# Second attention: the place of the weighted-values matmuls within a step of four scores

## What is computed

```
q, k = rope(h @ Wq), rope(h @ Wk);  v = h @ Wv
scores = q k^T / 4, masked so that row i sees columns <= i
ctx    = softmax(scores) @ v        # softmax subtracts the row maximum
```

## Time and profile before

| | |
|---|---|
| median of 3 runs | 4165.04 us (4164.26 to 4166.23) |
| profiled execution | 4157.04 us, of it the span 4155.2 us |
| PE busy | 3078.5 us, 74% |
| DVE busy | 2298.0 us, 55% |
| ACT busy | 1675.9 us, 40% |
| exponentials of the second attention (L660) | 1536, busy 693.8 us |
| reductions of the maxima (L925) | 1024, busy 733.9 us |
| weighted values (L1254) | 3072 matmuls, busy 327.3 us |

### The profile page before, as it was taken

The page is one execution under the profiler, slowest core; times in us unless marked ns, Lnnn a source line. Parts: engine busy times, 40 slices in busy tenths (PEclk is TensorE's granted clock), DMA queues, the critical chain, the costliest instruction groups (busy, mean ns, idle before and its releaser), DMA issues. The chain is left out here.

```text
span 4155.2 us, 54042 instructions
## 1 busy us (share of the span) xinstructions
PE 3078.5 (74%) x17636; PEld 1799.8 (43%) x17637; DVE 2298.0 (55%) x4488; ACT 1675.9 (40%) x3702; POOL 1106.6 (27%) x972
## 2 busy tenths in 40 slices
PE   5588558765965696579657955885587599999991
PEld 3444434343434443443444343444343366666660
DVE  4775567466837672866386557755675122222225
ACT  2456254525542554256335624562455122222223
POOL 6310630072016202420332053106200222222222
PEclk9789789887988898889788988997789799999995
DMA  1000000000000000000000000000000533333335
GB/s 55 11 11 12 22 21 2 13 20 21 2 30 3 21 2 32 0 21 2 32 1 21 2 32 11 12 12 22 11 2 11 185 55 55 55 61 56 55 53 167
DMA packets 85960, 125.57 MB, mean 30 GB/s; under 512 B 11600, under 2 KB 70864, under 8 KB 83664
## 3 DMA queue, kind: packets, MB, share of 16 engines
q1 hardware_dynamic: 59216, 85.40, 6.5%
q0 software_dynamic: 26496, 37.01, 5.0%
HBM read 58.23 MB, written 63.36 MB: 29 GB/s over the span
## 5 line engine op out<-in xcount | busy, mean ns | idle before, releaser
L660 ACT ACTIVATE PR<-SP_ 128x512 f32<-128x512 f32 (+3 forms) x1536 | 693.8, 489 | 457.8 <-PE SP_ L1241 310.9
L925 DVE TENSOR_REDUCE NM<-MX 128x1 f32<-128x128 f32 (+7 forms) x1024 | 733.9, 752 | 231.2 <-PE MX L1210 221.0
L421 POOL DMA_INDIRECT scratch_xs<-FX,SLOT x128 | 123.7, 967 | 1467.1 <-issue 1465.5
L439 POOL TENSOR_TENSOR work<-QK,VS 128x2048 f32<-128x2048 f32 x128 | 466.6, 3670 | 136.4 <-DVE QK L774 136.2
L1238 PE MATMUL SP_<-work,KST 99*128 99x512 bf16 (+3 forms) x1536 | 469.0, 333 | 44.1 <-ACT PR L660 32.2
L1208 PE MATMUL MX<-KST,work 96*128 96x512 bf16 (+3 forms) x1536 | 442.8, 353 | 70.0 <-DVE NM L925 58.5
L1503 POOL DMA_INDIRECT scratch_h<-Y,XG x136 | 210.6, 1548 | 617.1 <-DVE Y L1566 522.9
L1544 DVE TENSOR_TENSOR AG<-UB,SL 128x512 f32<-128x512 f32 x136 | 94.0, 691 | 476.3 <-PE UB L1583 476.3
L1254 PE MATMUL OA<-PR,V 128*32 128x512 f32 (+3 forms) x3072 | 327.3, 498 | 3.3 <-ACT PR L660 3.3
L1521 ACT ACTIVATE SL<-GB 128x512 f32<-128x512 f32 x136 | 81.2, 597 | 602.3 <-PE GB L1583 602.3
L818 DVE TENSOR_REDUCE AT<-work 128x256 f32<-128x4096 f32 x64 | 282.9, 4420 | 2.2
(11 more groups left out here) (253 smaller groups left out, 5092.7 us busy)
## 6 DMA issues: line engine op xcount, KB each, us to landing
XG<-scratch_xs SPq DMA_DIRECT2D x136, 130.0 KB, 2.1
X<-in_L_attn_x SPq DMA_DIRECT2D x8, 1024.0 KB, 5.6
scratch_x<-X SPq DMA_DIRECT2D x8, 1024.0 KB, 3.9
scratch_h<-A SPq DMA_DIRECT2D x8, 1024.0 KB, 3.9
X<-scratch_x SPq DMA_DIRECT2D x16, 512.0 KB, 4.0
HH<-scratch_h SPq DMA_DIRECT2D x16, 512.0 KB, 4.5
out<-X SPq DMA_DIRECT2D x16, 512.0 KB, 3.1
wg<-in_L_ffn_Wg SPq DMA_DIRECT2D x1, 4096.0 KB, 16.7
```

Source lines behind the costliest of these rows:

```text
L439: sg["prod1"].by(pool.tensor_tensor(P1[t % 2][:, i * hh * D:(i + 1) * hh * D].rearrange("p (h e d) -> p h e d", h=hh, e=HD), QK[:, t % 3, ...
L660: sg["exp"].by(act.activation(PR[:, n % 8, q0:512], SP_[:, n % 2, q0:512], ACT.Exp))
L925: sg["mx"].by(dve.tensor_reduce(NM[:, qt, h:h + 1], src, AX.X, ALU.max, negate=True))
```

## The change

The call of `weighted_values` in PE's list moves from behind the step's second score, ahead of the quarter M1, to behind its fourth score, ahead of M3. Before, the order in a step is: score, M0, score, weighted values, M1, score, M2, score, M3. After it, it is: score, M0, score, M1, score, M2, score, weighted values, M3. No other list changes and nothing is added or removed; the lists of DVE, ACT and SP are as they were.

```diff
                     for h in range(G):
                         scores(u, kt, h)
-                        if h == 1 and k >= 1:
+                        if h == 3 and k >= 1:
                             weighted_values(k - 1, *order[k - 1])
                         maxima(actions[n * h // G:n * (h + 1) // G])
```

## The result

The changed kernel takes 4326.75 us (median of 4 runs, 4325.24 to 4328.85) against 4164.94 us before, a ratio of 1.0387 with a 95% interval of 1.0375 to 1.0399. The direction was as predicted, the size was not: +162 us where +52 was forecast, and far above the range.

What follows compares the result with a forecast made beforehand. Bound by the PE-ACT-PE round with two score banks, and PE-DVE-PE where crowded. Terms (a) to (e) sum to +6.5 us per batch, x 8 = +52, giving 4209 profiled and 4217 us median; range 4172 to 4248.

Steps and rivals of the forecast that it cites:

- What bounds the kernel, and a step's length: Second attention: bound by the PE-ACT-PE round with two score banks, plus PE-DVE-PE where crowded; 2.88 us per step without maxima.
- The closed form: Step after: 1.89 + 1.00 + M3 + turn-over + M0 and M1's excess above 0.66 us; equal to before without maxima.
- (c): Units' first steps: DVE's copy of the sum, and reductions queued behind it, come later and PE waits; +6.8 us per batch.
- (e): Last step: its weighted values leave the gap where ACT idles and lie beside the last exponentials; -0.5 us per batch.
- (b): Units' second steps: the turn-over's four transposes now share the weighted values' gap and cost their full length; +1.9 us per batch.
- The clock: PE through the phase: keeps the full 2.4 GHz although waits grow to at most 1.4 us; nothing added.
- Rival D: The clock falls for some 8 steps a batch at some 1.2 us each: 77 us more, 4294 us; chance 0.05.
- (d): Steps where DVE idled for pieces: M1 and M2 no longer stand behind the weighted values; -3.45 us per batch.
- (a): Steps with a large piece, mostly in M3: it now shares the weighted values' gap; +1.75 us per batch.
- The prediction's own sign of being wrong: Phase not 4 to 10 us longer: the copy's delay is taken up, or (d) is far greater than in step 6.

Runs made afterwards that it cites:

- e1: Changed kernel with six extra matmuls on PE behind the weighted values of steps 4, 16 and 28; 4275.51 us, ratio 1.0298.
- e9: Changed kernel with six extra matmuls in steps 4, 16 and 28, and six ahead of M1 in steps 13 and 25; 4271.23 us, ratio 1.0260.
- e3: Kernel before, weighted values moved behind the fourth score only in the first step of each unit but the first; 4247.41 us, ratio 1.0221.
- e4: Kernel before, weighted values moved behind the fourth score in all steps but the first of each unit; 4219.04 us, ratio 1.0157.
- e5: e4 with the turn-over moved from the end of a unit's second step to behind M1 of that step; 4195.60 us, ratio 1.0069.
- e2: Kernel before with six extra matmuls behind the weighted values of steps 4, 16 and 28; 4185.19 us, ratio 1.0072.
- e7: Changed kernel with the weighted values behind the third score in every step, half the move; 4278.28 us, ratio 1.0273.
- e6: e4 with M3 ahead of the weighted values instead of behind them; 4194.82 us, ratio 1.0066.
- e10: Kernel before with the first action of each two-action step moved from M1 to M2; 4146.16 us, ratio 0.9950.

## Why the prediction was wrong, point by point

*What bounds the kernel, and a step's length*: right. The round without maxima is 2.88 us, step 41 of the first batch 3.38 where 3.32 was predicted; steps 17 and 29 at full clock are 3.76 (e1, e9) where the closed form gives 1.89 + 1.00 + 0.44 + 0.44 = 3.77. The closed form is for steps whose queues hold no other wait, and most of what follows is about those.

*(c), DVE's copy and what is queued behind it, +6.8*: right in place, too small in one part. (c) counted for steps 13 and 25 also M3 and the turn-over behind the weighted values, so e9 is its measure, with the whole move and the clock up: +7.9 us, of it 1.25 in step 4, 2.41 in steps 12 and 13 (for 1.7), 1.34 in step 16, 1.53 in 24 and 25, 1.34 in 28. e3 has 6.6 without that stacking; e4 has 1.0 for steps 13 and 25 alone, of which e5 takes back 0.6 with the turn-over.

*(e), the last step, -0.5*: right, -0.4 in step 47 and -0.2 in the two before.

*(b), the turn-over, +1.9*: right in kind (e5), too small: the steps named there are 2.9 us longer in e4 and 2.8 in e9. The closed form's lengths for the kernel before run over those of its trace in steps 17 and 29 (3.22 against 2.96), and I took the difference of two formulas where one of the two could be read.

*The clock, "so I take nothing for it"*: the step that failed most. It cost 7.3 us a batch, 58 us over the kernel, shown by e1 against e2, by e9 and by the last batch's step 17. Nearly all of it lies in steps 4, 5, 16, 17, 29, 41 and 42 (changed kernel less e9). My argument was that PE already waits for DVE up to 1.0 us without losing the clock, so that 1.4 wouldn't either. The waits came out at 1.95 us in step 4 and 1.54 in steps 16 and 28. And waits that are tolerated where they stand say nothing about others elsewhere: e7's fall comes behind a wait of 0.95 us. These runs agree in kind with the rule that I had quoted and set aside, from the Trainium skill, "TensorE: Matmul & The Clock Gate", section "HAM oscillation — how this bites in real kernels": granted clock 0.51 to 0.53 behind the three waits, though the case told there has longer waits, for DMA. Rival D named the mechanism, was priced at 77 us and given 0.05; it was near in price (77 for 58 us), partly by luck, for it reckoned some 8 steps at 1.2 us where three or four long steps a batch cost 1.0 to 2.4 each, and far off in chance.

*(d), pieces that come one block sooner, -3.45*: the second step that failed; all its steps together are +0.2 in e4. Steps 6 and 8 came as reckoned (-0.75 for -0.8, -1.06 for -0.95). But 1 to 3 gave +0.75 for -0.6, 10 +0.44 for -0.3, 19 and 31 +0.40 for -0.35 each. I moved M1 and M2 ahead of the weighted values and saw what they no longer wait for; I didn't look at what stands before them. M3 of the step before now comes behind the weighted values, and no long block is left between it and M1 to hide DVE's reduction of 0.8 to 1.2 us. e6 shows it: with M3 ahead of the block these waits go. But the gains of steps 6 and 8 go with them (+0.1 and -0.2 against the kernel before), and all of (d)'s steps together are -0.5 there: neither order gives the 3.45.

*(a), a large piece beside the weighted values, +1.75*: the steps named are +3.0 in e4, and four that I took as unchanged (11, 22, 34, 35) +1.5, of which step 34's 0.83 is the wait of (d) and not the gap's content.

Together, with the order's parts read from e9: 7.3 for the clock, 3.6 for (d), 1.3 for (a) and 1.5 for its missing steps, 0.9 for (b), 1.1 for (c), less 0.1 in (e): 15.6, which are the 15.6 us a batch between 6.5 and 22.1. That the clock and the two halves of the order add up is shown by e9. The split within the order is read from the steps; of its parts only the turn-over (e5) and M3's place (e6) were tried by themselves. The prediction's own sign of being wrong came true, a phase not 4 to 10 us longer; but both causes that it named for that would have made the kernel faster than forecast.

## What to carry to other kernels

In a PE queue that feeds two partners, a block's place decides what it hides on both sides: ask of each neighbour not only what it no longer waits for but what it now follows. When a change adds waits of 1 us and more on TensorE, price the microseconds behind them at half clock as a likely case, not as a remote one; here a wait of 0.95 us had a fall behind it and one of 0.98 had none. If extra matmuls in a wait make a kernel faster, the clock is the first suspect (look at the granted clock behind the wait); and the same matmuls in the kernel before are the control.

## What the runs showed of the hardware that was not expected

Eighteen useless matmuls a batch shortened the phase of the changed kernel by 5.8 us and lengthened that of the kernel before by 2.4. Behind one and the same wait of 1.54 us in step 16 the clock fell in seven batches and stayed up in the eighth. Time outside the second attention varies although that code is the same: between the end of one phase and the next first score it is 247.2 to 259.3 us over all profiles here (251.8 to 252.0, 248.6 and 255.8 within the kernel before), and the first score of the first batch lies at 235.5 to 244.4 us. The longest of these stretches, over 255 us, have 123 to 133 us at the lower clock, the shortest, up to 249.6, have 95 to 105; in between the order is loose. So the last 0.2% of such a kernel may depend on where in the rest the clock happens to fall, and e10's gain beyond its 7 us may be that; no run here tries it.
